# Matmuls of constants at the waits of a four-layer hybrid network kernel (one core of a Trainium2 chip)

## The reference, cut to what matters

```
x = x + deformable_conv(group_norm(x))                  # 9 taps
x = L1(x)        # convolution, 2-D Fourier transform, a gate, two 2x2 softmaxes, inverse transform, abs
t = tokens(x)                                           # 8 x 256 x 32
t = t + nystrom_attention(layer_norm(t))                # 16 landmarks, 6 pseudo-inverse steps, 33-wide residual
t = t + experts(layer_norm(t))                          # 16 experts, softmax over tokens, the 8 best of each
t = t + linear_attention(layer_norm(t))                 # 4 layers of 8 heads
t = t + routed(layer_norm(t))                           # up to 33 steps; h[0,0,:19] picks the operation of a step
```

## Time and profile before

| what | us |
|---|---|
| median of 3 executions without profile | 355.32 |
| lowest and highest of them | 354.33, 356.91 |
| the profiled execution's own time | 352.09 |
| its span, first to last instruction | 350.3 |
| PE busy in it | 295.9 (84%) |
| DVE, ACT, POOL busy in it | 196.1, 158.8, 39.1 |

### The profile page before, as it was taken

One profiled execution on the slowest core, in us unless ns is written; L12 is line 12 of the kernel. 1 busy time (PEld: TensorE's weight loads), 2 busy tenths in 40 slices (PEclk: granted clock), 3 DMA queues, 4 the chain that ended last, 5 costly groups with the idle time before them and its releaser, 6 DMA issues.

```text
span 350.3 us, 6471 instructions
## 1 busy us (share of the span) xinstructions
PE 295.9 (84%) x1952; PEld 193.5 (55%) x1952; DVE 196.1 (56%) x460; ACT 158.8 (45%) x341; POOL 39.1 (11%) x37
## 2 busy tenths in 40 slices
PE   8999999999885888988999778977867877777872
PEld 3665777775432467987997346666622453225510
DVE  4686998864177665788766533411331493226620
ACT  1097677774361356354561241111024285445930
POOL 5200090001000050005200000242000000000001
PEclk9999999999998999999999996999895899989988
DMA  3954200000000000000000222231000000000000
GB/s 86 242 97 102 67 0 2 2 2 2 0 0 0 1 2 0 2 0 1 0 2 0 46 59 59 63 58 44 0 1 6 17 0 0 17 17 0 0 0 30
DMA packets 9108, 8.98 MB, mean 26 GB/s; under 512 B 3932, under 2 KB 8668, under 8 KB 8796
## 3 DMA queue, kind: packets, MB, share of 16 engines
q1 hardware_dynamic: 8820, 8.39, 10.7%
q10 hardware_dynamic: 264, 0.30, 0.3%
HBM read 8.42 MB, written 0.26 MB: 25 GB/s over the span
## 4 chain that ended last, share of the span: by engine, by line
PE 61%; DVE 15%; ACT 9%; issue 7%; DMA 3%; DVEq 1%; SPq 1%; POOL 1%; POOLq 0%
PE ps L581 10%; PE ps L524 6%; PE ps L589 5%; PE ps L744 3%; DMA recA<-rec_a 3%; PE ps L750 3%; PE ps L543 2%; PE ps L879 2%; PE ps L732 2%; ACT arena L1218 2%; DVE rmax L1664 2%; PE ps L992 2%; PE ps L871 1%; ACT arena L1052 1%; PE ps L610 1%
## 5 line engine op out<-in xcount | busy, mean ns | idle before, releaser
L1338 DVE TENSOR_TENSOR arena<-arena 128x512 f32 x72 | 44.4, 689 | 7.8 <-ACT arena L1052 4.5
L524 PE MATMUL ps<-xC,cstb 128*128 128x512 f32 x94 | 47.6, 651 | 0.0
L1059 ACT ACTIVATE arena<-ps 128x512 f32<-128x512 f32 x72 | 37.7, 602 | 15.7 <-PE ps L581 15.6
L581 PE MATMUL ps<-cstb,arena 128*128 128x128 f32 x288 | 36.3, 277 | 0.7 <-DVE arena L1338 0.7
L581 PEld LDWEIGHTS ps<-cstb,arena 128*128 128x128 f32 x288 | 31.0, 140 | 9.4 <-DVE arena L1338 8.6
L524 PEld LDWEIGHTS ps<-xC,cstb 128*128 128x128 f32 x94 | 19.0, 213 | 25.8 <-issue 25.6
L589 PE MATMUL ps<-arena 128*32 128x256 f32 x288 | 19.2, 385 | 0.0
L744 PE MATMUL ps<-arena 128*128 128x160 f32 x96 | 15.3, 307 | 2.7 <-DVE arena L1522 1.5
L1218 ACT ACTIVATE arena<-ps,rmax 128x256 f32<-128x256 f32 x32 | 14.9, 471 | 5.2 <-DVE rmax L1664 5.2
L1237 ACT ACTIVATE arena<-ps,w2c 128x512 f32<-128x512 f32 x16 | 9.7, 688 | 15.6 <-PE ps L992 15.6
L744 PEld LDWEIGHTS ps<-arena 128*128 128x128 f32 x96 | 13.3, 190 | 3.8 <-DVE arena L1522 2.4
(11 more groups left out here) (371 smaller groups left out, 540.4 us busy)
## 6 DMA issues: line engine op xcount, KB each, us to landing
arena<-rec_a SPq DMA_DIRECT2D x19, 128.5 KB
toepb<-toep SPq DMA_DIRECT2D x1, 1536.0 KB
w32b<-w SPq DMA_DIRECT2D x1, 1225.0 KB
cstb<-cst SPq DMA_DIRECT2D x1, 1044.0 KB
recA<-rec_a SPq DMA_DIRECT2D x3, 128.5 KB
arena<-rec_b SPq DMA_DIRECT2D x19, 16.5 KB
w1b<-moe_w SPq DMA_DIRECT2D x1, 264.0 KB
xC<-x SPq DMA_DIRECT2D x1, 256.0 KB, 2.8
```

What stands on the lines that cost most here:

```text
L524: mm(ps[7], ident if lhs is None else lhs, xC if rhs is None else rhs, start=True, stop=True)
L581: last = tr(ps[c % BI][:, (q * PT + t) * P:(q * PT + t + 1) * P], ST[:, c, t, q * 8:q * 8 + 8, :], ident)
L1059: af(SQ[:, c].rearrange("p q n -> p (q n)"), ps[c % BI], ACT.Copy).then_inc(S["s_ev"], 1)
L1338: tt_(ST[:, c], hy.unsqueeze(3).to_broadcast([P, PT, 16, 16]), hx.unsqueeze(2).to_broadcast([P, PT, 16, 16]), ALU.mult).then_inc(S["prod"], 1)
```

## The change

`keep_busy` gets two parameters, the PSUM bank and the number of columns. Calls of it are added at twelve places in the text, at waits (three of them in `layer`, which runs four times; the third of these is behind the return of the last layer, so eleven calls are run there), and one call grows from 2 to 4. A wait for `q_ev` 2 is added at the landmarks, so that bank 1 is free. No work that feeds the output is added, moved or removed.

```
-            def keep_busy(count, lhs=None, rhs=None):
+            def keep_busy(count, lhs=None, rhs=None, bank=7, cols=512):
 
                 for _ in range(count):
-                    mm(ps[7], ident if lhs is None else lhs, xC if rhs is None else rhs,
+                    mm(ps[bank][:, 0:cols], ident if lhs is None else lhs, (xC if rhs is None else rhs)[:, 0:cols],
                        start=True, stop=True)
...
             last.then_inc(S["fft_mm"], 1)
 
+            keep_busy(4)
             pe.wait_ge(S["abs"], 2)
...
                    ).then_inc(S["v_mm"], 1)
+            pe.wait_ge(S["q_ev"], 2)
+            keep_busy(1, bank=1)
+            keep_busy(1, bank=1, cols=256)
             pe.wait_ge(S["ql_bd"], 1)
             pe.wait_ge(S["kl_bd"], 1)
...
                ).then_inc(S["xT_mm"], 1)
+            keep_busy(1, bank=7, cols=256)
             for half in range(2):
                 pe.wait_ge(S["xT_ev"], half + 1)
...
             last.then_inc(S["mT_mm"], 1)
+            keep_busy(1, cols=256)
             pe.wait_ge(S["moe_ev"], MOE_EV["mT"])
...
             last.then_inc(S["pl_mm"], 1)
+            keep_busy(1, cols=256)
             pe.wait_ge(S["moe_ev"], MOE_EV["pl"])
...
             last.then_inc(S["hid_mm"], 1)
+            keep_busy(1, cols=384)
             pe.wait_ge(S["hid_ev"], 1)
...
             last.then_inc(S["hid_mm"], 1)
+            keep_busy(1, cols=384)
             pe.wait_ge(S["moe_ev"], MOE_EV["hidT"])
...
             last.then_inc(S["eo_mm"], 1)
+            keep_busy(1, cols=256)
             mm(ps[7][:, 0:C], cst_("rep16")[0:EXP, :], b2b, start=True, stop=False)
             pe.wait_ge(S["moe_ev"], MOE_EV["eo"])
             mm(ps[7][:, 0:C], eo, ident[0:C, 0:C], start=False, stop=True).then_inc(S["eoT_mm"], 1)
+            keep_busy(1, bank=6, cols=256)
             pe.wait_ge(S["moe_ev"], MOE_EV["eo_bd"])
...
             def layer(l, last_one):
+                keep_busy(1, bank=0, cols=256)
                 pe.wait_ge(S["la_gev"], l + 1)
...
                    start=True, stop=False)
+                keep_busy(1, bank=0, cols=256)
                 pe.wait_ge(S["la_hevA"], l + 1)
...
                 last.then_inc(S["la_t"], 1)
+                keep_busy(1, bank=0, cols=256)
                 pe.wait_ge(S["la_pev"], l + 1)
...
             to_C(T, 0, S["ct_mm"])
-            keep_busy(2)
+            keep_busy(4)
             pe.wait_ge(S["ct_ev"], 4)
             pe.wait_ge(S["op_ev"], 1)
```

## The result

| | kernel before | changed kernel |
|---|---|---|
| median of 20 executions each | 355.34 | 351.88 |
| lowest, highest | 351.93, 366.97 | 349.45, 355.94 |
| mean of the 20 | 356.2 | 352.3 |
| the profiled execution, its span | 352.09, 350.3 | 351.43, 349.6 |
| mean granted clock of the profiled execution | 0.954 | 0.968 |

By the medians of all executions the change is worth 1.0%, by the means 1.1%.

What follows compares the result with a forecast made beforehand. The prediction saw a row of small hand-overs, TensorE holding 61% of the chain, its clock dipping after waits. Gains 3.3 less costs 1.1 gave 2.2, plus 2.1 at the median: 355.32 to 351.0 us, range 347.8 to 354.6.

Steps and rivals of the forecast that it cites:

- line of 351.8: Whole kernel: a measurement tells about 1%, 3.55 us, from no change; below this line counts as faster, chance 0.54.
- Gate: Fourier gate: four calls in a 3.59 us wait cost nothing; matmuls behind run at full clock, gain 0.7 us.
- Landmarks: Landmark stage: added calls cost 0 to 0.2 us, taken 0.1; no gain in the profiled execution.
- Experts: Expert stage: six calls keep the clock up, gain 1.8 us; cost 0 to 0.5, taken 0.2.
- Layers: Linear attention: three calls per layer cost 0.8 us in all; L913 at higher clock, 0.5 credited of 0.9.
- First step: First routed step: two more calls in a 4.80 us hole; gain 0.3 credited of 1.05, cost nothing, bounds -1.05 and +1.7.
- From the profile to the median: Median lies 3.2 us above the profiled execution; 2.1 taken as half clock in stages that get matmuls.
- B: Rival: narrow fillers do not hold the clock, or dips move or gains are hidden; 354.3 us, chance 0.26.
- C: Rival: fillers in layers and experts run at half clock and slow the kernel; 359.6 us, chance 0.08.
- A: Rival: clock stays up in all touched stages in every execution; 348.8 us, chance 0.16.

Runs made afterwards that it cites:

- experts alone: Only the six calls in the expert stage added to the kernel before; median 353.5 against 353.9, ratio 0.999.
- layers alone: Only the three calls in `layer` (linear attention) added to the kernel before; median 356.4 against 353.9, ratio 1.011.
- first of the pruned versions: Changed kernel without third layer call, L844 call and landmark calls; 128 columns at L832, 8 calls before first routed step; median 350.2, ratio 0.984.
- landmarks alone: Only the three calls at the landmarks, with the wait for `q_ev`, added to the kernel before; median 355.2, ratio 1.001.
- thin calls: Changed kernel with all its added calls 8 columns wide instead of 256 to 512; median 355.9, ratio 1.001.
- pruned, second version: First pruned version plus one 384-column call ahead of the wait for ct_ev 2, and 3 instead of 4 calls behind the logits; median 352.6, ratio 0.995.
- gate alone: Only the four calls ahead of the wait for abs 2 added to the kernel before; median 363.9 against 353.9, ratio 1.014.
- first step alone: Kernel before with only the call ahead of the first routed step grown from 2 to 4; ratio 1.000.

## Why the prediction was right or wrong

The forecast was 351.0 us, in the range of 347.8 to 354.6; the median is 351.88. The gain of the median, 3.5 us, came out a fifth smaller than the forecast 4.3, and just on the far side of the line of 351.8, where I had seen the smaller chance. The nearness is in part luck. In the profiled execution the forecast was -2.2 us and the measured difference of the times is -0.7; from there to the median it was -2.1 and came out at -2.8. The two misses have opposite signs. By stages:

**Gate.** Forecast -0.7 us, measured -0.65, in the way described: VectorE became late. In two other profiles without these calls (experts alone, layers alone) L652 to L665 took 10.7 to 10.8 us, since the dip was longer there. So the same calls save up to 1.8. One sign that I had named for being right failed: the clock was not at 1.00 from 105 to 130 us, and the dip behind the gate took 0.92 us back at L666, which the sum did not hold.

**Landmarks.** Forecast +0.1, measured 0: L679 started 0.16 us behind the end of VectorE's copy, before the change 0.14. The ledger's +0.92 is the dip at L666, ahead of these calls.

**Experts.** Forecast -1.8 + 0.2, net -1.6; measured -1.40 + 0.18, net -1.22. The gains held: L841 -0.57 (0.55), L846 to L849 -0.25 (0.25), L849 -0.95 (1.0). The costs were mis-sized, 0.5 us instead of 0.2. The call ahead of L844 cost 0.35 rather than 0.1 to 0.2: VectorE's copy ended at 213.52, L856 started at 213.93; the first of the pruned versions, without this call, has L832 to D1573 shorter by 0.34. L832 came 0.17 late, which I had counted as covered: its wait was the shortest, 0.37 us; with 128 columns there the delay is gone.

**Layers.** Forecast +0.8 - 0.5, measured +0.43 - 0.92. I had priced the third call at 0.2 to 0.3 each time; it is 0.14. L902 did come 0.24 us later behind L892 (1.42 us against 1.18), as forecast, but its four passes, now right behind L897's, took 0.61 instead of 0.71 us. The gain at L913 is there in this pair of profiles, but it is not shown to come from the calls: landmarks alone, the thin calls and the kernel without any call in the layers had L913 at full clock too. In those two last kernels L860 to D1607 was 0.4 to 0.5 us shorter than in the changed one. What the calls in the layers do is cost 0.4 us and, by the times below, keep off the executions at half clock.

**First step.** Forecast -0.3, measured +1.55 and +0.29. This is the step that failed. I had weighed one danger, that the sequencer would wait for the passes, and had excluded it rightly. The clock gain (0.3) did not come with four calls and does come, in full, with eight. And TensorE's first branch took 1.43 us longer, which no term of the sum held. The passes are excluded as its cause by three runs: two more calls alone leave it at 0.35, two calls fewer leave it at 1.96, the thin calls, with next to no work in the array, have 0.88. In all kernels with 60 to 96 added instructions it was between 0.46 and 2.18 us, in all with 24 or fewer it was 0.35 or 0.36. The profile has a queue for loads of instructions, and between 258 and 266 us it had this in the kernel before and in the changed one:

```profile
q8 instruction: 1, 0.02, 0.8%
```

```profile
q8 instruction: 2, 0.03, 1.6%
```

Over the whole execution both kernels have 13 loads of this queue, of 16 KB each; what differs is when they come. The trace has the start and the length of each. For the eight kernels with 60 or more added instructions, the last load that starts before the branch (us):

| kernel | load starts, ends | branch starts, ends | branch | from the load's end to the branch's end |
|---|---|---|---|---|
| no call in the layers | 259.29, 260.53 | 259.78, 261.96 | 2.18 | 1.43 |
| two calls at the first step | 259.08, 260.07 | 259.53, 261.50 | 1.96 | 1.43 |
| changed kernel | 259.93, 261.08 | 260.73, 262.51 | 1.78 | 1.43 |
| no third call in a layer | 259.17, 260.29 | 260.73, 261.67 | 0.94 | 1.38 |
| thin calls | 261.49, 262.41 | 262.97, 263.85 | 0.88 | 1.44 |
| eight calls at the first step | 258.34, 259.26 | 260.07, 260.70 | 0.62 | 1.44 |
| pruned, first version | 257.57, 258.82 | 260.51, 260.97 | 0.46 | 2.15 |
| pruned, second version | 256.31, 257.60 | 259.23, 259.69 | 0.46 | 2.09 |

In the six kernels with 24 or fewer, the last load before the branch had started more than 30 us earlier, and the branch took 0.35 or 0.36 us. So where the branch is long it ends 1.4 us behind the end of a load, whatever its own start, and it is short where the load was over more than 1.6 us before it began. The branch waited for something that this load brought; that it is the code behind the branch is an inference, since the trace does not say what a load holds and no run moved the code alone.

**From the profile to the median.** I had put 2.1 of the 3.2 us between the profiled execution and the median down to stages that get matmuls, with the layers at half clock as the candidate. The size was near, 2.8 us: the median of the kernel before lies 3.2 us above its profiled execution, that of the changed kernel 0.45. The mechanism was not the one named. I had reasoned with a layer's worth, about 4 us. It is 3.64 a layer, and in both traces that caught it (gate alone, first step alone) the clock, once down, stayed down from 228 to 266 us, so it cost 11 us. Such executions are the far end of the times, and a median does not see them. What is seen in the other traces, one execution of each of the fourteen kernels, is this (thin calls count as none):

| stage | without calls there | with them |
|---|---|---|
| L652 to L665, gate | 9.66 to 10.78 (6 kernels) | 9.02 or 9.03 (8) |
| L818 to D1573, experts | 11.18 to 12.29 (6) | 9.44 to 9.97 (8) |
| L860 to D1607, layers | 28.31 to 29.46, and 40.5 twice (7) | 28.41 to 29.26 (7) |
| L934 to the end, never any | 74.31 to 77.67 (14) | |

The kernel before was profiled near its best in the first two rows (9.67 and 11.18): against these six kernels the changed one saves 0.6 to 1.8 and 1.2 to 2.3 us, and the calls make the stage nearly the same each time. That is up to 2.2 us more than the ledger of the two profiles has. So the stages that get matmuls do hold gains that this pair of profiles hides, but at the gate and in the experts; how much of the 2.8 us they are is not shown, since no execution near the median of the kernel before was profiled. The last row shows how much of a difference between two single profiles means nothing.

The calls in the layers are for the far end. Over all runs of this study the kernel before was above 359 us in 19 of 120 executions, 2 of 20 in the comparison above. Kernels that had 256 columns at least at two waits of each layer were there in 1 of 80, at 361.1; the kernel that lacked only those calls in 2 of 12, and all kernels without them, the one before included, in 33 of 187. The mean sees this: 19/120 of 11.2 us is 1.8 us, an estimate, nearly half of the 3.9 us by which the means differ. It takes each of the 19 as a loss of the layers, which is seen in two traces of other kernels and not in these; their times run from 359.5 to 372.9 us, so they are not all one and the same loss.

**Rivals.** B, that dips move or hide behind VectorE, describes this profile in part: a dip appeared at L666 and cost 0.92 us. C, fillers at half clock, was not seen in an added call, but in calls that had stood there before: the four behind L813 ran at half clock in three of the fourteen traces (experts alone, layers alone, and the changed kernel without the third call) and cost 1.5 us each time. A would have needed the first step; with eight calls there the median was 350.3, still above its 348.8.

The sentence of the Trainium skill (TensorE: Matmul & The Clock Gate, What's actually happening) that the ramp costs less than 1% of a typical kernel fits the size of this change's gain (0.8% by the ratio, 1.0% by the medians), but not a clock that stays down: 11.2 us of 350 are 3.2%. Its section Why this matters for your kernels warns of long idle gaps between bursts of matmuls. These runs show that short ones are enough: in the layers of the gate-only kernel the clock fell at 228.2 us and stayed down with no wait of TensorE above 0.62 us there.

## What to carry to other kernels

Fill waits of TensorE with wide constants only up to the length of the wait: 256 columns in a wait of 0.37 us cost 0.17, a call with no wait of its own cost 0.14 to 0.35 each time, and a hole filled by half bought nothing where a full one bought 1.2 us. Judge such a change by many executions and by their mean, because what it prevents may be rare and large, and one profile can show none of it. And look at the first branch behind the place where you added code, with the loads of instructions beside it: 80 more instructions made it 1.43 us longer here, more than the gate or the layers gave.

## What was not expected of the hardware

- In the layers the clock stayed at half for 37.6 us, although TensorE showed busy for 83 to 94% of each 5 us. In the same stage at full clock, in the kernel before, it showed 70 to 81% and kept the clock. So the same work ran at either of the two clocks.
- With every added matmul 8 columns wide the dips at the gate and in the experts were as before; with the same instructions 256 to 512 columns wide they were gone.
- The same branch of the same program text took between 0.35 and 2.18 us, by what stood in front of it in the program, and where it was long it ended 1.38 to 1.44 us behind a load of instructions.
